# Opening loads, causal keys, reciprocals and context scores moved in a kernel of stacked attention stages

## The reference, cut to what matters

```python
# block L0: context attention        x = layer_norm(x + attn(x, ctx), ...)
# block L1: causal self-attention    x = layer_norm(x + attn(x, x, causal=True))
#           context attention        x = layer_norm(x + attn(x, ctx))
#           mixture of 8 experts, top 2
# block L2: quantised self- and context attention, gated feed-forward
# block L3: grouped-query attention on the context (64 features a head), feed-forward
Q = (q_in @ wq + bq).reshape(Bq, Sq, H, HD)
Kp = (k_in @ wk + bk).reshape(Bq, Sk, H, HD)
V = (v_in @ wv + bv).reshape(Bq, Sk, H, HD)
scores = jnp.einsum('bqhd,bkhd->bhqk', Q, Kp) / jnp.sqrt(jnp.float32(HD))
if causal:
    mask = jnp.tril(jnp.ones((Sq, Sk), bool))
    scores = jnp.where(mask, scores, -jnp.inf)
a = jax.nn.softmax(scores, axis=-1)
o = jnp.einsum('bhqk,bkhd->bqhd', a, V).reshape(Bq, Sq, Dm)
return o @ wo + bo
```

## Time and profile before

| | us |
|---|---|
| timed runs, median of 3 | 1946.06 |
| timed runs, each | 1929.76, 1946.20, 1946.06 |
| profiled execution, its own time | 1932.07 |
| its span, first to last instruction | 1929.9 |

### The profile page before, as it was taken

One profiled execution on the slowest core, in us unless ns is written; L12 is line 12 of the kernel. 1 busy time (PEld: TensorE's weight loads), 2 busy tenths in 40 slices (PEclk: granted clock), 3 DMA queues, 4 the chain that ended last, 5 costly groups with the idle time before them and its releaser, 6 DMA issues.

```text
span 1929.9 us, 31362 instructions
## 1 busy us (share of the span) xinstructions
PE 1515.2 (79%) x10849; PEld 886.7 (46%) x10912; DVE 1120.1 (58%) x3101; ACT 893.6 (46%) x2282; POOL 638.9 (33%) x1171
## 2 busy tenths in 40 slices
PE   0678778888877789999778777676668777877889
PEld 0344335544533347777544444344445433444445
DVE  1455556665555643332588888977775455454433
ACT  0334425444533345543466666666673233443351
POOL 4111000000100000111378787776672234343320
PEclk9889989999999999999865666755558889999989
DMA  5212220231052100000200000000000000000000
GB/s 146 43 41 40 51 55 25 53 61 30 12 128 44 35 1 1 1 1 1 87 1 1 1 2 2 1 1 2 2 1 1 1 1 7 1 8 1 1 2 22
DMA packets 32440, 44.07 MB, mean 23 GB/s; under 512 B 9772, under 2 KB 25756, under 8 KB 29980
## 3 DMA queue, kind: packets, MB, share of 16 engines
q1 hardware_dynamic: 27664, 40.39, 9.3%
q10 hardware_dynamic: 4620, 1.69, 0.4%
HBM read 33.73 MB, written 8.32 MB: 22 GB/s over the span
## 4 chain that ended last, share of the span: by engine, by line
PE 51%; DVE 18%; POOL 12%; issue 10%; ACT 7%; DMA 1%; SPq 1%; POOLq 0%; ACTq 0%; DVEq 0%
POOL arena L1878 8%; PE trans L958 6%; PE score L947 6%; ACT arena L1274 4%; PE acc L919 4%; DVE minus_top L1612 3%; PE trans L896 2%; PE trans L892 2%; DVE arena L1434 2%; PE misc L838 2%; PE misc L767 2%; PE acc L917 2%; PE score L1086 2%; PE score L858 2%; PE trans L1049 2%
## 5 line engine op out<-in xcount | busy, mean ns | idle before, releaser
L1274 ACT ACTIVATE arena<-score,minus_top,exp_scale 128x512 f32<-128x512 f32 (+1 forms) x512 | 315.9, 624 | 178.5 <-POOL minus_top L1863 178.5
L1612 DVE TENSOR_REDUCE minus_top<-score 128x4 f32<-128x616 f32 (+4 forms) x256 | 198.0, 806 | 188.2 <-PE score L868 85.5
L1878 POOL TENSOR_SCALAR arena<-arena,inv_total 128x512 f16<-128x512 f32 (+1 forms) x512 | 281.1, 549 | 47.6 <-DVE inv_total L1682 8.7
L1768 POOL TENSOR_TENSOR rstd<-spread,minus_half 128x4 f32<-128x4 f32 x36 | 36.7, 1020 | 749.4 <-DVE spread L1354 663.1
L1240 ACT ACTIVATE arena<-trans 128x512 f32<-128x512 f32 x240 | 141.9, 597 | 186.1 <-PE trans L896 182.0
L1675 DVE TENSOR_REDUCE top_score<-score 128x2 f32<-128x1024 f32 (+1 forms) x192 | 206.2, 1074 | 0.8 <-PE score L988 0.8
L988 PE MATMUL score<-arena 32*128 32x512 bf16 (+1 forms) x512 | 98.1, 431 | 131.7 <-ACT arena L1274 127.7
L1312 ACT ACTIVATE arena<-arena,minus_top 128x154 f32<-128x154 f32 x256 | 105.1, 412 | 193.9 <-DVE minus_top L1740 193.7
L1004 PE MATMUL trans<-ident_half,arena 128*128 128x128 f16 x1536 | 185.3, 295 | 2.5 <-POOL arena L1878 2.5
L1004 PEld LDWEIGHTS trans<-ident_half,arena 128*128 128x128 f16 x1536 | 137.6, 133 | 67.0 <-POOL arena L1878 47.8
L1251 ACT ACTIVATE arena<-score,b_cols 128x512 f32<-128x512 f32 x128 | 86.9, 687 | 112.5 <-PE score L947 112.0
(11 more groups left out here) (254 smaller groups left out, 2949.7 us busy)
## 6 DMA issues: line engine op xcount, KB each, us to landing
arena<-q_terms SPq DMA_DIRECT2D x192, 64.0 KB
q_terms<-arena SPq DMA_DIRECT2D x36, 128.0 KB
late<-k_terms SPq DMA_DIRECT2D x64, 64.0 KB
arena<-k_terms_ctx SPq DMA_DIRECT2D x128, 20.0 KB
late<-in_L_xattn_e_w SPq DMA_DIRECT2D x1, 2048.0 KB, 14.3
k_terms<-arena SPq DMA_DIRECT2D x12, 128.0 KB
attn_w<-in_attn_w SPq DMA_DIRECT2D x1, 1280.0 KB, 5.7
arena<-in_mask_Bx1xSxS_ff SPq DMA_DIRECT2D x4, 308.0 KB, 5.0
```

What stands on the lines that cost most here:

```text
L1274: ins = nc.scalar.activation(probs[:, i % 2, j, of], score[i % 2][:, j, of], ACT.Exp, bias=minus_top[:, at_col:at_col + 1], scale=exp_scal ...
L1612: nc.vector.tensor_reduce(dst, src, axis=AX.X, op=ALU.max, negate=True).then_inc(top_ready, 1)
L1878: ins = nc.gpsimd.tensor_scalar(codes[:, (i - 1) % 2, j, of], probs[:, (i - 1) % 2, j, of], inv_total[:, at_col:at_col + 1], HALF_ROUND, A ...
```

## The change

Five parts. (1) SP loads first the seven tensors that unit 0 needs and counts the other eight apart; ACT issues six DMAs instead of 36, the context coming padded and reordered from the host; DVE waits for POOL's clearing first and for seven loads later; POOL adds two rows of biases (before: DVE). (2) In unit 0 the stacks of K are read back by ACT's queue, and the stacks of Q in two parts, the first two pairs of heads by themselves; the feed-forward loads come after them. (3) K of unit 4, the first causal one, is made in unit 2 (slot f+9), and SP doesn't hold its stacks for unit 3's start. (4) ACT copies the sums of N1 out of misc, and DVE inverts them in place in four pieces of 128, items "r", in slots f+5 to f+8; N2, W, M and H move to f+9, f+10, f+12 and f+14. (5) In a context group the four steps stand in slots 0, 1 and 2 (one, one and two), and "tops" in slot 4. Line numbers of the changed kernel are its own.

```diff
@@ -119,7 +119,8 @@
-    a, b = (min(PER_GROUP[v], PER_GROUP[v] * m // (PER[u] - 3)) for m in (n, n + 1))
+    last = PER[u] - (2 if is_cross(u) else 3)
+    a, b = (min(PER_GROUP[v], PER_GROUP[v] * m // last) for m in (n, n + 1))
...
-    before = [("ctx", 0), ("x", 0), ("pads", 0), ("K", 0), ("Q", 0), ("kt", 0)]
+    before = [("ctx", 0), ("pads", 0), ("x", 0), ("K", 0), ("Q", 0), ("kt", 0)]
...
             if u:
                 at(exact, f + 4, ("N1", u - 1))
-                at(exact, f + 6, ("N2", u - 1))
-                at(exact, f + 7, ("W", u - 1))
-                at(exact, f + 9, ("M", u - 1))
-                at(exact, f + 11, ("H", u - 1))
+                for n in range(4):
+                    at(exact, f + 5 + n, ("r", u - 1, n))
+                at(exact, f + 9, ("N2", u - 1))
+                at(exact, f + 10, ("W", u - 1))
+                at(exact, f + 12, ("M", u - 1))
+                at(exact, f + 14, ("H", u - 1))
             if nxt in EXACT_UNITS:
-                at(exact, f + 2, ("K", nxt))
+                if nxt == SELF * B - 1:
+                    at(exact, f + 9, ("K", nxt + 1))
+                if nxt != SELF * B:
+                    at(exact, f + 2, ("K", nxt))
                 at(exact, f + 3, ("Q", nxt))
                 if is_cross(nxt):
                     at(exact, f + 12, ("kt", nxt))
         else:
             at(exact, f + 4, ("V", u))
             at(exact, f + 3, ("N1", u - 1))
-            at(exact, f + 6, ("N2", u - 1))
-            at(exact, f + 7, ("W", u - 1))
-            at(exact, f + 10, ("M", u - 1))
-            at(exact, f + 13, ("H", u - 1), ("cna", u))
+            for n in range(4):
+                at(exact, f + 5 + n, ("r", u - 1, n))
+            at(exact, f + 9, ("N2", u - 1))
+            at(exact, f + 10, ("W", u - 1))
+            at(exact, f + 12, ("M", u - 1))
+            at(exact, f + 14, ("H", u - 1), ("cna", u))
...
-                at(exact, f + g * per + per - 2, ("tops",) + next_group(u, g))
+                at(exact, f + g * per + per - (1 if is_cross(u) else 2), ("tops",) + next_group(u, g))
...
-            items = [(0, "B", 12), (0, "N1", 11), (1, "N2", 11), (2, "W", 11), (4, "M", 11), (5, "H", 11)]
+            items = [(0, "B", 12), (0, "N1", 11), (2, "r", 11, 0), (2, "r", 11, 1), (3, "r", 11, 2), (3, "r", 11, 3),
+                     (4, "N2", 11), (5, "W", 11), (6, "M", 11), (7, "H", 11)]
...
-                     (norm_sel, io["norm_sel"]), (rows[:, :, :], io["rows"].partition_broadcast(P)),
+            loads = [(ident[:, :], io["ident"]), (sizes[:, :], io["sizes"].partition_broadcast(P)), (cols[:, :], io["cols"]),
                      (causal_f, io["causal"]), (causalT_f, io["causalT"]), (head_mask[:, :], io["head_mask"]),
-                     (expert_no[:, :], io["expert_no"]), (sizes[:, :], io["sizes"].partition_broadcast(P)),
-                     (b1_cols[:, :], io["b1_cols"]), (ffb_cols[:, :], io["ffb_cols"]),
-                     (router_w[:, :], io["L1_xattn_router_w"]),
-                     (router_b[:, :], io["router_b"].partition_broadcast(P))]
+                     (attn_w[:, 0:4, :], io["attn_w"][:, 0:4, :])]
+            late_loads = [(rows[:, :, :], io["rows"].partition_broadcast(P)), (norm_sel, io["norm_sel"]),
+                          (attn_w[:, 4:20, :], io["attn_w"][:, 4:20, :]), (expert_no[:, :], io["expert_no"]),
+                          (b1_cols[:, :], io["b1_cols"]), (ffb_cols[:, :], io["ffb_cols"]),
+                          (router_w[:, :], io["L1_xattn_router_w"]),
+                          (router_b[:, :], io["router_b"].partition_broadcast(P))]
...
                     sp.dma_start(dst, src).then_inc(weights_in, 16)
+                for dst, src in late_loads:
+                    sp.dma_start(dst, src).then_inc(late_in, 16)
...
-                for b in range(B):
...
-                    for j in range(4):
-                        act.dma_start(pad_col[32 * j:32 * j + CTX_TAIL, b, 1:2], col_dram[P:CTX, one])\
-                            .then_inc(seq_in[b], 16)
+                for b, loaded in ((slice(0, 1), first_seq_in), (slice(1, B), rest_in)):
+                    act.dma_start(ctx_in[:, b, :, :], io["ctx"][:, b, :, :]).then_inc(loaded, 16)
+                    act.dma_start(x[:, b, :, :], x_dram[:, b, :, :]).then_inc(loaded, 16)
+                    if loaded is first_seq_in:
+                        act.dma_start(pad_rep.rearrange("p b k -> p (b k)"),
+                                      io["mask_BxS2_ff1"].rearrange("b k -> (b k)").partition_broadcast(P))\
+                            .then_inc(loaded, 16)
+                        act.dma_start(pad_col, io["pad_cols"]).then_inc(loaded, 16)
...
-                dve.wait_ge(weights_in, 16 * len(loads))
-                dve.wait_ge(cleared, 3)
+                dve.wait_ge(cleared, 4)
...
+                dve.wait_ge(weights_in, 16 * len(loads))
...
-                for dst, src in [(e_b2[:, :], io["L1_xattn_e_b2"]), (ff_w1[:, :], io["L2_xattn_ff_w1"]),
-                                 (ff_w2[:, :, :], io["L2_xattn_ff_w2"].rearrange("(c p) d -> p c d", p=P))]:
-                    sp.dma_start(dst, src).then_inc(ff_in, 16)
...
-                        if u >= 2:
+                        if u >= 2 and not (u == SELF * B and side == "k"):
 
                             sp.wait_ge(scoresT_ready, FIRST_SLOT[u - 1])
                         if u == SELF * B and side == "k":
                             sp.wait_ge(k_half_cleared, 1)
+                        if u == 0 and side == "k":
+
+                            continue
+                        if u == 0:
+
+                            for s in range(2):
+                                for n, term in enumerate(terms):
...
+                                    sp.dma_start(q_stack[r, 0, 0:2, :], terms_of[s * HD:(s + 1) * HD, term, 0:2, :])\
+                                        .then_inc(q_first, 16)
+                        pairs = slice(0 if u else 2, PAIRS)
                         for s in range(2):
                             for n, term in enumerate(terms):
                                 r = slice(s * STACK + n * HD, s * STACK + (n + 1) * HD)
-                                dst = keys[r, s, :, :] if side == "k" else q_stack[r, u % 2, :, :]
-                                sp.dma_start(dst, terms_of[s * HD:(s + 1) * HD, term, :, :]).then_inc(stacked, 16)
+                                dst = keys[r, s, :, :] if side == "k" else q_stack[r, u % 2, pairs, :]
+                                sp.dma_start(dst, terms_of[s * HD:(s + 1) * HD, term, pairs, :]).then_inc(stacked, 16)
+                    if u == 0:
+                        for dst, src in [(e_b2[:, :], io["L1_xattn_e_b2"]), (ff_w1[:, :], io["L2_xattn_ff_w1"]),
+                                         (ff_w2[:, :, :], io["L2_xattn_ff_w2"].rearrange("(c p) d -> p c d", p=P))]:
+                            sp.dma_start(dst, src).then_inc(ff_in, 16)
...
-                        pe.wait_ge(q_stacked, 32 * len(Q_TERMS) * (u + 1))
+                        if u:
+                            pe.wait_ge(q_stacked, 32 * len(Q_TERMS) * (u + 1))
+                        else:
+                            pe.wait_ge(q_first, 32 * len(Q_TERMS))
                         if stage(u) == L0:
                             pe.wait_ge(pad_ready, u + 1)
+                    if u == 0 and i == PER_GROUP[0]:
+                        pe.wait_ge(q_stacked, 32 * len(Q_TERMS))
...
+                    elif name == "N1":
+                        if u == 0:
+                            act.wait_ge(late_in, 16 * LATE_LOADS)
+                        act.wait_ge(misc_raised, m + 1)
+                        if u:
+                            act.wait_ge(misc_read, out_of("N2", u - 1))
+                        nc.scalar.copy(inv_sum, misc[:, :]).then_inc(misc_read, 1)
...
+                act.wait_ge(k_out, 48)
+                for s in range(2):
+                    for n, term in enumerate(K_TERMS):
+                        r = slice(s * STACK + n * HD, s * STACK + (n + 1) * HD)
+                        act.dma_start(k_half_ctx[r, 0, s, :, :], k_terms_ctx.ap()[s * HD:(s + 1) * HD, term, :, :])\
+                            .then_inc(k_stacked, 16)
...
-                        dve.wait_ge(misc_raised, m + 1)
-                        nc.vector.reciprocal(inv_sum, misc[:, :]).then_inc(misc_read, 1)
+                        if u == 0:
+                            dve.wait_ge(late_in, 16 * LATE_LOADS)
+                    elif name == "r":
+                        dve.wait_ge(misc_read, out_of("N1", u))
+                        of = slice(n * P, (n + 1) * P)
+                        nc.vector.reciprocal(inv_sum[:, of], inv_sum[:, of]).then_inc(sums_inverted, 1)
                     elif name == "N2":
                         dve.wait_ge(misc_raised, m + 1)
-                        dve.wait_ge(misc_read, out_of("N1", u))
```

(13 more changed lines are left out.)

59 lines of the change are left out of this document (26 added, 33 removed).

## The result

The changed kernel takes 1952.6 us (median of 19 runs, 1936.3 to 1959.5) against 1939.5 for the kernel before, measured beside it (19 runs): a ratio of 1.0067, 95% interval 1.0042 to 1.0091. I had said 1903, faster. The profiled execution took 1950.0 us with a span of 1948.2.

What follows compares the result with a forecast made beforehand. Bounds named: ACT's loads, one queue's chain to first scores, PE's waits for stacks and inversion, otherwise nearly PE. -20.8 + 3.5 + 5.8 - 9.7 - 10.8 + 2.8 = -29.2 from 1932.1 gives 1903 us, range 1880 to 1928.

Steps and rivals of the forecast that it cites:

- The beginning: Start up to the first scores: fewer loads and DMAs, K's reads on ACT; first scores at 30.4, -21.3 us.
- The beginning gives back: Rival, chance 0.12: K's and Q's reads share engines, +4.9, and the rest of Q lands 3 us late; 1911.
- Unit 0: First unit: keeps its hole, the longer chain shows once, +0.5; unit 1 starts 20.8 us earlier.
- Units 1 to 3: Context units after the first: +3.5, +5.8 and -9.7 us.
- Units 8 to 11: Later context units: first group +1.6, second -2.0, third +0.5, fourth +0.6; four units +2.8 us.
- Part 5, context groups: Plain context group goes from 7.85 to 8.9 us, +1.1; groups without the pad matmul +0.6.
- Part 4, the inversion: Unit 1's groups with the inversion in four pieces: +2.6, -2.9, +2.6, +1.1; unit 1 +3.5 us, unit 2 +5.8.
- The clock: Rival, chance 0.08: PE's new pauses before "tops" let the granted clock fall; +24, 1927 us.
- Causal units: V no longer waits, -3.6 each; maxima not behind W, -0.8; second group +1.7; four units -10.8 us.
- Part 3: Unit 3's fourth group loses its hole, 21.3 to 11.0 us, -10.3; unit 3 -9.7.
- Slower: Rival, chance 0.04: the maxima's way out lies wholly behind the weighing in every context group, 3.3 us each; 1965.
- Three slots do what two did not: Rival, chance 0.12: spreading steps removes most of PE's 33.9 us waits for maxima, way out hides; 1879.

Runs made afterwards that it cites:

- experiment 3: Parts 1 and 2 of the change alone, on the kernel before: 1920.3 us, ratio 0.9926.
- experiment 2: Part 5 of the change alone, on the kernel before: 1979.1 us, ratio 1.0225.
- experiment 4: Parts 1, 2 and 3 of the change, without 4 and 5, on the kernel before: 1909.5 us, ratio 0.9893.
- experiment 10: Changed kernel without part 5, Q's terms written out before K's stacking, q's first two pairs stacked separately in every context unit: 1848.0 us, ratio 0.9561.

## Why the prediction was wrong

By the profiled executions 1903 stands against 1950.0. The forecast put the end of the exact stage 29.2 us earlier, at 667.2; it came at 710.0. (The stages behind took 4.7 more than before, which says nothing of the edit.) The 42.8 us between, by the prediction's own steps:

- **The beginning: +3.9 of the 42.8.** The seven loads landed for DVE at 10.69, where I had taken half of 15.16, 7.6, so the block ended 3.4 later (12.3 for 8.9). I scaled a landing time by the number of loads, though the one with the weights came last. Q out came 4.5 behind K out (I said 3.9), Q's reads 5.0 behind that (4.15), the scores 6.9 behind those (7.1). Moving K's reads to ACT's queue did most of what the row had said: ACT issued its first at 21.61, and Q out followed at 22.66 and not 5.4 us after the start of K's reads as in the earlier trace rows. Beside K's reads it then took 5.0 instead of 4.15, so 0.85 were given back. The Trainium skill (DMA: Bandwidth & Descriptors, "Issuing engines are not separate DMA queues") calls the sequencer's time that a second issuer saves usually small; for these reads of 20 KB it was not. The rival "The beginning gives back" is out as a whole, since experiment 3 keeps 18 us; its second half came in part: PE waited 2.7 us for the rest of Q, where I had taken 0.5.
- **Unit 0: +2.9.** It took 52.5 us for 49.6. Its first group alone is 3.8 longer than before, that wait of 2.7 included; 0.5 had been allowed.
- **Units 1 to 3: +13.8** (54.6, 57.9, 52.6 for 49.7, 52.2, 49.4). **Units 8 to 11: +19.9** (195.8 for 175.9). Here failed the steps "Part 5, context groups" and "Part 4, the inversion": the sums of the waits were right and PE's clock in them wrong. The groups of the changed kernel that ran at 1.00 throughout took what the two steps add up to: unit 1's second 11.3 (11.3), unit 3's first 14.9 (14.8) and second 11.3 (11.4), the second of units 8, 9 and 11 10.5 (10.5). The others, with the clock below 1.00, are longer but for unit 8's first. In unit 9 the steps gave 15.2, 10.5, 11.3, 7.9 and the kernel took 16.3, 10.5, 12.5, 9.5; with two pauses filled, the last two are 11.5 and 8.0. The plain group of unit 1 took 10.2 for 8.9, and 8.8 with fillers and a full clock. These seven units had 91 us at 1.2 GHz, 41 before. At half speed 91 us lose at most 46, by estimate, so the clock is enough for the 33.7 of excess; how much of them is its own was not measured in sum. The rival "The clock" had this mechanism and its tell ("if PE's clock falls in context units"), at a chance of 0.08 and +24. Exact stage at 1.2 GHz: 116 us for 71.
- **Causal units: +2.4.** Their second group takes 16.0 where I had 13.6 + 1.7 = 15.3, in each of four; the first 20.9 to 22.3 as said.
- **Part 3** removed the hole as said: unit 3's last group fell from 21.3 to 12.5 us, where I had 11.0 (its clock stood at 1.2 GHz for 3.4 us).

I had argued the clock's chance down with "none of 2 us in these rows did it". That misread the rows. The window at 0.88 in the earlier trace rows is unit 1's second group before, and its longest pause is this one:

```profile
127.07 0.31 PE L858 MATMUL score<-arena 128*128 128x154 bf16 x1 [2.18 <-DVE minus_top L1612]
```

The same matmul had taken 0.23 us before the pause and took 0.34 from just behind it, so the clock fell with a pause of 2.2 us and none longer since the hole of unit 0. It was also a sentence on single pauses: in the changed kernel nearly every context group has two to four of them, of 0.5 to 3.0 us, where a plain group before had none. The Trainium skill (TensorE: Matmul & The Clock Gate, "A second HAM failure mode: psum-queue depth-cycling") tells, right behind the case that I cited, of a kernel whose engine idled only briefly between groups of matmuls while it cycled through its output banks, and whose clock swung as well. The trace agrees with that case, and I had weighed only the other. Which pauses bring the clock down stays open: second groups with pauses of 1.9 and 0.8 us kept 1.00.

There is a second mistake that the total hides. Parts 3 and 4 are worth 27.8 us, parts 1 and 2 18.1, and part 5 costs 59.5, where I had 1.1 and 0.6 a group, 27 us over its 32 context groups. Unit 9's second group shows it at full clock in all three kernels: 12.5 before, 8.8 with part 4 and without part 5, 10.5 with both. So part 4 gives 3.7 there and part 5 costs 1.6. My 10.5 had 0.6 in it for part 5 and so 2.6 for part 4; it was right because both were too small by about as much, which is luck, and hid that part 5 was the part to leave out. Steps in two slots had little left that three could gain once part 4 was there (waits of 4.8 us). But that explains no more than 11 us of part 5's price, since without part 4 it cost 48.3. The rival "Slower" comes nearest in the sum: it decided from 2.1 us a group on, and 59.5/32 is 1.9; its tell, plain groups of 10 us or more, came true (10.2 in unit 1), but at full clock the same group takes 8.8. I gave it 0.04. "Three slots do what two did not" is out: in experiment 2 the spread steps did take the wait of 33.9 us away, and the kernel was slower.

## What to carry to other kernels

Before a step is spread to relieve a wait, ask what in the waited-for engine's row stands in front: here one inversion of 3.4 us made 37 us of waits (experiment 4), and cutting it into four (with its items' slots, part 4) took 23.5 us off the stage, while spreading the steps and delaying the handover cost 60. A handover through another engine (maxima, split, transposition, copy) needs PE work behind its last input and again behind the transposition; work placed ahead of its input covers nothing. When a stage becomes shorter, its transfers become the next hole, and splitting them so that the first group's operands come first was worth more than issuing them earlier.

## What the runs showed of the hardware

Short pauses bring TensorE's clock down as a long one does: with one wait of 4.0 us and none other over 3.0, 116 of 667 us ran at 1.2 GHz; in the kernel of experiment 10, with fewer pauses and none over 1.9 us once the first exponentials are past, 9 of 569, all of them before 52 us. A filler matmul in a real pause paid for itself where the clock came up with it (12.5 to 11.5 and 9.5 to 8.0 us in two groups of unit 9), and not where it didn't (unit 10); one behind the pause instead of in it cost its own length (10.5 to 11.4 us at full clock). And 16 reads of 64 KB from one queue took 10.7 us from the last issue to the scores; with half the bytes first, the scores had nothing to wait for 5.6 us after the last issue (560.76 + 5.34 against 571.72).
